# A decoder layer on one core: the feed-forward's products in plain fp32 in place of sums of fp32r parts, last normalisation shared by ACT and DVE

## The reference, cut to what matters

```python
logits = jnp.clip(xt @ gate_w.T, -50.0, 50.0)
top_w, top_idx = jax.lax.top_k(logits, 2)
rw = jax.nn.softmax(top_w, axis=-1)
deltas = jax.nn.softmax(expert_atom_weights, axis=-1) @ atoms
weighted = deltas * jax.nn.sigmoid(importance)          # 8 experts x 2048
rows, cols = mask_idx // H, mask_idx % H                # 2048 indices
vals = jnp.einsum('tk,tks->ts', rw, weighted[top_idx])
contrib = jax.ops.segment_sum((xt[:, cols] * vals).T, rows, num_segments=H)
out = xt @ W.T + contrib.T
x = _layernorm(x + out)
```

## Time and profile before

| | us |
|---|---|
| median of 3 runs | 961.38 (958.9 to 964.02) |
| the profiled execution's own time | 964.11 |
| its span in the profile | 962.3 |
| cross attention, last batch | about 850 to 884 |
| feed-forward phase | 886.3 to 962.3 |
| mean granted clock, share of 2.4 GHz | 0.959 |

### The profile page before, as it was taken

One profiled execution on the slowest core, in us unless ns is written; L12 is line 12 of the kernel. 1 busy time (PEld: TensorE's weight loads), 2 busy tenths in 40 slices (PEclk: granted clock), 3 DMA queues, 4 the chain that ended last, 5 costly groups with the idle time before them and its releaser, 6 DMA issues. The chain is left out here.

```text
span 962.3 us, 19095 instructions
## 1 busy us (share of the span) xinstructions
PE 876.3 (91%) x7675; PEld 760.0 (79%) x7675; DVE 564.5 (59%) x1073; ACT 551.5 (57%) x948; POOL 85.7 (9%) x96
## 2 busy tenths in 40 slices
PE   5944689999999999999999999999999999997875
PEld 3533479898889888988898889898989898976654
DVE  2796455656565656565656565656565656565764
ACT  2512166757576657665666566656665667565322
POOL 1021000000000000000000000000000000016577
PEclk8966799999999999999999999999999999999997
DMA  6009566675757575757575757575757575454042
GB/s 177 12 30 265 148 136 161 133 176 128 177 117 181 126 181 119 177 127 179 118 178 127 179 118 178 128 178 118 179 125 181 117 178 107 97 145 127 20 118 75
DMA packets 70262, 133.32 MB, mean 139 GB/s; under 512 B 24096, under 2 KB 53448, under 8 KB 70088
## 3 DMA queue, kind: packets, MB, share of 16 engines
q1 hardware_dynamic: 66240, 123.61, 54.1%
q0 software_dynamic: 2048, 7.34, 2.8%
q10 hardware_dynamic: 1888, 1.15, 0.4%
HBM read 52.59 MB, written 5.57 MB: 60 GB/s over the span
## 5 line engine op out<-in xcount | busy, mean ns | idle before, releaser
L1267 ACT ACTIVATE probsT<-ps_T 125x448 f32<-125x448 f32 x384 | 195.1, 544 | 176.4 <-PE ps_T L1141 176.3
L1370 DVE CUSTOM_DVE_ANT_0 scores<-ps_scores,mask_sb 112x1500 f32<-112x1500 f32 x128 | 219.7, 1716 | 79.0 <-PE ps_scores L1130 71.1
L1141 PEld LDWEIGHTS ps_T<-ident,scores 112*125 112x125 f32 x1536 | 199.9, 188 | 18.9 <-ACT probsT L1267 4.7
L1141 PE MATMUL ps_T<-ident,scores 112*125 112x112 f32 x1536 | 207.5, 271 | 2.9 <-ACT probsT L1267 2.7
L1257 ACT ACTIVATE scores<-scores,shift 112x1500 f32<-112x1500 f32 x128 | 197.1, 1540 | 1.5 <-DVE shift L1370 1.5
L1118 PE MATMUL ps_proj<-wkvT,room 128*125 128x256 f32 x1152 | 159.7, 289 | 5.9 <-DVE v_sb L1348 5.9
L1110 PE MATMUL ps_proj<-room,wkvT 128*128 128x500 f32 x576 | 157.2, 409 | 5.5 <-DVE room L1353 3.8
L1155 PE MATMUL ps_out<-probsT,v_sb 125*32 125x112 f32 x3072 | 159.6, 260 | 0.0
L1118 PEld LDWEIGHTS ps_proj<-wkvT,room 128*125 128x125 f32 x1152 | 146.8, 189 | 14.7 <-DVE v_sb L1348 6.1
L1155 PEld LDWEIGHTS ps_out<-probsT,v_sb 125*32 125x32 f32 x3072 | 144.2, 110 | 15.5 <-issue 10.7
L1357 DVE SCALAR_TENSOR_TENSOR room<-ps_proj,xbk,room 128x500 fp32r<-128x500 f32 x96 | 70.8, 738 | 125.6 <-ACT room L1252 125.6
(11 more groups left out here) (254 smaller groups left out, 561.7 us busy)
## 6 DMA issues: line engine op xcount, KB each, us to landing
k_stack<-room SPq DMA_DIRECT2D x384, 187.5 KB, 4.0
ctx_rows<-in_ctx SPq DMA_DIRECT2D x48, 500.0 KB
mask_sb<-in_mask_BxSxS_ff SPq DMA_DIRECT2D x32, 328.1 KB
q_stack<-q_hi SPq DMA_DIRECT2D x32, 112.0 KB, 5.4
q_hi<-k_stack SPq DMA_DIRECT2D x4, 448.0 KB, 3.8
q_lo<-k_stack SPq DMA_DIRECT2D x4, 448.0 KB, 4.0
q_stack<-q_lo SPq DMA_DIRECT2D x16, 112.0 KB, 5.4
x_sb<-in_x SPq DMA_DIRECT2D x1, 896.0 KB, 6.9
```

Source lines behind the costliest of these rows:

```text
L1141: last = nc.tensor.transpose(ps_T[0:LT, (TB * t + k) % 2, j * PN:(j + 1) * PN], scores[:, t % 2, (k * TC + j) * LT:(k * TC + j + 1) * LT], ...
L1267: nc.scalar.activation(probsT[:, t % 2, k * TC:(k + 1) * TC], ps_T[0:LT, (TB * t + k) % 2, 0:TC * PN].rearrange("p (j n) -> p j n", j=TC), ...
L1370: nc.vector.tensor_tensor_reduce(out=split(scores[:, t % 2], NC), in0=ps_scores[0:PN, :, 0:LC], in1=split(mask_sb[:, a], NC), scale=-1.0, ...
```

## The change

- The high and low parts of `W`, of the gate weights, of the transposed tokens and of `prod` are gone. `wT`, `gateT`, the tokens `x2T` and `prod` are plain fp32, and `pick_r` is read as fp32. `scatter` has two products in place of four, `dense` four in place of twelve, the logits two in place of six.
- ACT's rounding copies, POOL's and DVE's low parts, and the two low parts of weights at the start of the cross attention (DVE) are gone. T is one DVE copy; ACT stores the tokens once it is done. In the last batch of the cross attention that store stands behind the next probability copies.
- POOL's gathers of the second half stand directly behind the power of the last tile.
- `centre` is a `scalar_tensor_tensor` with `rstd` broadcast as second operand.
- The last normalisation: DVE computes `shift = -mean * rstd` (`shifted`), ACT centres the four tiles of the first half and two of the second with it, DVE the other two. The output goes in three stores: the first half and two tiles from SP's queue, two tiles from ACT's.

The core of the diff:

```diff
     elif u == ("L", 0, 0):
-        (hi, lo), g_hi, g_lo = x2T_parts(keep, h), keep["gateT_hi"], keep["gateT_lo"]
-        mm = [t for m in range(KT) for t in ((g_hi[:, m], hi[:, m]), (g_hi[:, m], lo[:, m]), (g_lo[:, m], hi[:, m]))]
-        for n, (g, x) in enumerate(mm):
-            last = nc.tensor.matmul(bank[0:E, 0:HALF], g, x, start=n == 0, stop=n == len(mm) - 1)
+        for m in range(KT):
+            last = nc.tensor.matmul(bank[0:E, 0:HALF], keep["gateT"][:, m], x2T_of(keep, h)[:, m], start=m == 0, stop=m == KT - 1)
...
     elif kind == "T":
-        dve.wait_ge(k["x2T_hi_ready"], KT * h + p + 1)
-        hi, lo = x2T_parts(keep, h)
-        nc.vector.tensor_tensor(lo[:, p], bank[:, 0:HALF], hi[:, p].bitcast(F32), ALU.subtract).then_inc(out, 1)
+        nc.vector.tensor_copy(x2T_of(keep, h)[:, p], bank[:, 0:HALF]).then_inc(out, 1)
...
-    nc.vector.tensor_scalar(keep["x1"][:, tile], keep["resid"][:], keep["mv"][:, 0:1], keep["rstd"][:, bass.ds(tile, 1)],
-                            ALU.subtract, ALU.mult).then_inc(keep["r_steps"], 2)
+    nc.vector.scalar_tensor_tensor(out=keep["x1"][:, tile], in0=keep["resid"][:], scalar=keep["mv"][:, 0:1],
+                                   in1=keep["rstd"][:, tile:tile + 1].broadcast_to([TT, D]),
+                                   op0=ALU.subtract, op1=ALU.mult).then_inc(keep["r_steps"], 2)
...
             def _(pool):
                 nc.gpsimd.memset(keep["c_stack1"][:].bitcast(F32), 0.0).then_inc(keep["stack_cleared"], 1)
-                for n in range(NST):
-                    low(n)
-                    if n == POW_AT:
-                        result_on_gpsimd(nc, pool, keep, NT - 1)
+                result_on_gpsimd(nc, pool, keep, NT - 1)
                 pool.wait_ge(keep["x2T_stored"][1], 16)
                 for j in range(NST):
                     pool.wait_ge(prod_ready, j + 1)
                     gather_on_gpsimd(nc, pool, io, keep, 1, j)
-                for n in range(NST, len(UNIT)):
-                    low(n)
...
-                        mm = [t for k in range(KT) for t in ((wT_hi[:, k, e], x2T_hi[:, k]), (wT_hi[:, k, e], x2T_lo[:, k]),
-                                                             (wT_lo[:, k, e], x2T_hi[:, k]))]
-                        for n, (w, x) in enumerate(mm):
-                            nc.tensor.matmul(ps[:, 4 + 2 * h + m, 0:HALF], w, x, start=n == 0, stop=False)
+                        for k in range(KT):
+                            nc.tensor.matmul(ps[:, 4 + 2 * h + m, 0:HALF], wT[:, k, e], x2T_of(keep, h)[:, k], start=k == 0, stop=False)
...
                 def scatter(n):
                     h, j = UNIT[n]
-                    wait_lo(pe, n)
+                    pe.wait_ge(prod_ready, n + 1)
                     for m in range(KT):
-                        for part in (prod_hi, prod_lo):
-                            last = nc.tensor.matmul(ps[:, 4 + 2 * h + m, 0:HALF], pick_r[:, j, m * P:(m + 1) * P], part[:, n % BUFS],
-                                                    start=False, stop=j == NST - 1 and part is prod_lo)
+                        last = nc.tensor.matmul(ps[:, 4 + 2 * h + m, 0:HALF], pick[:, j, m * P:(m + 1) * P], prod[:, n % BUFS],
+                                                start=False, stop=j == NST - 1)
                     last.then_inc(contributed, 1)
...
+                def centred(h, which):
+                    act.wait_ge(shift_ready, h + 1)
+                    for i in which:
+                        nc.scalar.activation(y_sb[:, i], resid3[:, i], ACT.Identity, scale=rstd[:, i:i + 1], bias=shift3[:, i:i + 1]).then_inc(y_ready[2 * h], 1)
+                copied(0)
+                centred(0, tiles(0))
                 copied(1)
+                centred(1, tiles(1)[HT // 2:])
+                act.wait_ge(y_ready[2], HT // 2)
+                store(act, tiles(1)[HT // 2:])
...
                         if n >= BUFS:
-                            wait_lo(dve, n - BUFS)
+                            dve.wait_ge(contributed, n - BUFS + 1)
                         nc.vector.tensor_tensor(prod[:, n % BUFS], ps[:, 2 + n % 2, 0:HALF], xg[j], ALU.mult).then_inc(prod_ready, 1)
-                        if n > 0:
-                            low(n - 1)
```

More of the change, by code:

```diff
@@ L649, in load_indices, with store_transposed @@
                  allow_slow_non_contiguous=True).then_inc(keep["idx_col_in"], 16)
-def store_transposed(act, io, keep, h):
-    act.wait_ge(keep["x2T_full"], KT * (h + 1))
-    act.dma_start(io["x2T"][h].rearrange("(m p) t -> p m t", p=P), expert_room(keep)["x2T"][:, KT * h:KT * (h + 1)]).then_inc(keep["x2T_stored"][h], 16)
+def store_transposed(act, io, keep, h, out, out_value):
+    act.wait_ge(out, out_value)
+    act.dma_start(io["x2T"][h].rearrange("(m p) t -> p m t", p=P), x2T_of(keep, h)).then_inc(keep["x2T_stored"][h], 16)
 def gather_on_gpsimd(nc, pool, io, keep, h, j):
@@ L772, in late_unit_on_vector @@
     k = keep
-    if kind in "RL" and read:
+    if kind in "RTL" and read:
         dve.wait_ge(in_psum, in_value)
@@ L1288, in batch @@
                         probs_out(2 * d + 1)
+                        if at is AT_LAST and d == 0:
+                            store_transposed(act, io, keep, 0, unit_out, units_before(half, a) + AT_LAST[("T", KT - 1, 0)] + 1 + 2)
                         next_exponentials(2 * d)
@@ L1594, in feed_forward_phase @@
         sem = lambda n: ctx.enter_context(nc.semaphore(n))
[L1595 to L1596 removed]
         keep["c_stack1"] = sb("c_stack1", [P, HALF], F32R)
         e = expert_room(keep)
[L1599 to L1600 removed]
+        pick, xg = e["pick_r"].bitcast(F32), e["xg"]
+        wT, w_stack, x2 = (keep[n] for n in ("wT", "w_stack", "x1"))
         prod = sb("prod", [P, BUFS, HALF])
[L1602 to L1603 removed]
         ffT = sb("ffT", [P, KT, T])
@@ L1626, in feed_forward_phase @@
         rstd_ready = sem("rstd3_ready")
-        y_ready = [sem(f"y_ready{h}") for h in range(2)]
+        shift_ready = sem("shift3_ready")
+        y_ready = [sem(f"y_ready{n}") for n in range(3)]
         stored = keep["stored"]
@@ L1631, in tiles, with store @@
             return range(h * HT, (h + 1) * HT)
-        def on_pool(n):
-            return n < NST or n >= POOL_FROM
-        def lo_before(n, pool):
-            return sum(on_pool(k) == pool for k in range(n))
-        def wait_lo(engine, n):
-            if on_pool(n):
-                engine.wait_ge(lo_pool, lo_before(n, True) + 1)
-            else:
-                engine.wait_ge(lo_dve, lo_before(n, False) + 1)
+        def store(engine, which):
+            out = io["out"].rearrange("b s d -> (b s) d").rearrange("(i p) d -> p i d", p=TT)
+            engine.dma_start(out[:, which[0]:which[-1] + 1], y_sb[:, which[0]:which[-1] + 1]).then_inc(stored, 16)
         with nc.Block() as block:
@@ L1652, in _ @@
                 stack_shares(sp, keep, 1, late_out, len(HIDDEN))
-                for h in range(2):
-                    sp.wait_ge(y_ready[h], HT)
-                    sp.dma_start(io["out"].rearrange("b s d -> (b s) d").rearrange("(i p) d -> p i d", p=TT)[:, h * HT:(h + 1) * HT],
-                                 y_sb[:, h * HT:(h + 1) * HT]).then_inc(stored, 16)
-                sp.wait_ge(stored, 32)
+                sp.wait_ge(y_ready[0], HT)
+                store(sp, tiles(0))
+                sp.wait_ge(y_ready[1], HT // 2)
+                store(sp, tiles(1)[:HT // 2])
+                sp.wait_ge(stored, 48)
             @block.gpsimd
@@ L1691, in dense @@
                 def dense(h):
-                    x2T_hi, x2T_lo = x2T_parts(keep, h)
                     if h == 1:
@@ L1818, in normalise, with shifted @@
                     nc.vector.tensor_scalar(var_eps[:, g], mv[:, g, 1], LN_EPS, None, ALU.add).then_inc(var_ready, 1)
-                def centred(h):
+                def shifted(h):
+                    g = slice(h * HT, (h + 1) * HT)
                     dve.wait_ge(rstd_ready, h + 1)
-                    for i in tiles(h):
-                        nc.vector.tensor_scalar(y_sb[:, i], resid3[:, i], mv[:, i, 0:1], rstd[:, i:i + 1], ALU.subtract, ALU.mult).then_inc(y_ready[h], 1)
+                    nc.vector.scalar_tensor_tensor(out=shift3[:, g], in0=mv[:, g, 0], scalar=-1.0, in1=rstd[:, g], op0=ALU.mult, op1=ALU.mult).then_inc(shift_ready, 1)
                 def late(k):
                     late_unit_on_vector(nc, dve, keep, HIDDEN[k], 1, ps[:, k % 2], NT - 1, late_in_psum, k + 1, late_out, k + 1)
-                def low(n):
-                    if not on_pool(n):
-                        dve.wait_ge(prod_hi_ready, n + 1)
-                        if n >= BUFS:
-                            dve.wait_ge(contributed, n - BUFS + 1)
-                        nc.vector.tensor_tensor(prod_lo[:, n % BUFS], prod[:, n % BUFS], prod_hi[:, n % BUFS].bitcast(F32), ALU.subtract).then_inc(lo_dve, 1)
                 late(0)
@@ L1854, in _ @@
                             normalise(0)
```

(7 more changed lines are left out.)

97 lines of the change are left out of this document (24 added, 73 removed).

## The result

The changed kernel took 970.52 us (median of 4 runs, 968.51 to 972.87), the kernel before beside it 960.73 (4 runs): ratio 1.0087, 95% interval 1.0058 to 1.0117, so 8.4 us slower; the two medians are 9.8 us apart. The forecast was 967.1, 5.7 us more than the profiled execution of before; the time lies in the range given, and the sign is the forecast one. The profiled execution of the changed kernel has a span of 966.7 us, 4.4 more than that of before (own times 968.51 and 964.11; the first is the fastest of its runs, the second stands above its median, so the pair of profiles shows less than the medians do). Executions more than 1.5% above the fastest of their kernel are left out of every ratio and of the medians of the kernel before.

A forecast was written before the change was run, and what follows sets the result against it. No engine filled the feed-forward; its chain of waits did, and PE would fill it after the change. Terms 0.3 + 0.7 + 5.1 - 0.4 = +5.7 us on 961.4 gave 967.1 us, range 962.5 to 972.

The forecast's parts named there:

- The bound: Feed-forward to its last scatter: no engine fills it, waits do; after the change PE should run gapless.
- The price of a product: One plain fp32 128x448 product on PE: 0.753 us, taken from self-attention; each replaced fp32r pair costs 0.343 us more.
- The rival of 0.820: Plain fp32 products on PE take four fp32r passes, 0.820 us each, or loads show: 971.9 us; chance 0.12.
- the fast one of 0.376: Plain fp32 products on PE cost one record, 0.376 us, not two: 944 us; chance 0.05.
- 1, the last batch: Last batch of cross attention: logits go from six fp32r products to two fp32 ones on PE, +0.3 us.
- 2, to the end of `dense(0)`: Start of the feed-forward to the end of `dense(0)`: four fp32 products are 16 passes, +0.7 us.
- about 10 in the 3.7 us until the clock rises: In `dense(0)`: about 10 of 16 passes before the clock rises, 6 more at 0.188, 1.1 us.
- the clock rival: Feed-forward start: clock rise one step earlier costs 2 us less, 965 us; later, 969 us; chance 0.16.
- 3, to the last scatter: From the end of `dense(0)` to the last scatter: PE work 61.3 plus waits 1.0, 62.3 against 57.2, +5.1 us.
- The three checks of "gapless": PE up to the last scatter: gathers early, DVE's 3.14 us block covered by 3.4, no wait for PSUM or `prod` buffers.
- 4, the tail: After the last scatter: centrings split over DVE and ACT gain 0.4 us, stores still 3.2 us; -0.4 us.
- The hand-over of `shift`: After the last scatter: `shift` adds a small DVE operation and a hand-over, 0.2 us.

The follow-up runs named there:

- the second experiment: Changed kernel with scatter back to hi/lo fp32r products, high parts by ACT, all low parts by DVE, POOL only gathers and powers: 980.6 us, ratio 0.9951.

## Why the prediction came out as it did

*The bound.* Right. The kernel was filled by nothing and is now filled by PE (62.37 of 63.00 us). The rule of the sum, added PE work against waits that vanish, is what the runs bear out: with the scatter alone taken back to fp32r parts the loss turned into a gain, 11.0 us between the two in one group, and the intervals of the ratios (0.9933 to 0.9969, 1.0045 to 1.0084) are apart.

*The price of a product.* Right: 1.50 us for the two of a unit, 0.75 each, against 0.753 from the earlier trace rows. The rival of 0.820 is out, and so is the fast one of 0.376. The Trainium skill (FP8 and Floating Point Precision, TensorE Precision Notes) says four passes; the trace shows two records of 0.376 each for a product, against 0.205 for an fp32r product. So four passes at the fp32r pace don't give the time here: a quarter of 0.753 is 0.188, shorter than 0.205.

*1, the last batch* (+0.3). Wrong in what it covers. PE's last products there started 0.7 us later, at 881.59 instead of 880.90, but the phase began 0.8 us earlier. The sum took the gathers to be finished before the barrier and PE's end to set it. By the two lines of the last gather and the kernel before's second profile, the phase starts 3.4 to 3.6 us after the last issue each time, while PE waits: 2.93 us before, 1.41 now and 4.22 in the second profile of before. So PE's added 0.3 us could not show, and the term that counted, when POOL issues its last gather, stood in the sum at nothing. It moved by 2.0 us between two profiles of the kernel before, so the -0.8 need not be the change's.

*2, to the end of `dense(0)`* (+0.7). Wrong by 0.9: it took 7.5 us, not 8.4. The sum put the rise of the clock inside 893 to 894; the profile shows 0.69 in 890 to 891 and 1.00 from there. The step that failed is "about 10 in the 3.7 us until the clock rises". This is the clock rival (0.16), in one profile; it gave back less than the 2 us that I gave it. (The sum's own terms, 3.7 and 1.1, make 4.8; the 0.2 up to 5.0 is not worked out.) In the first group the changed kernel ran `dense(0)` at the full clock, 1.00 in each microsecond from 898 on, after a wait of 0.74 us at the barrier:

```profile
903.60 3.17 PE L1642 MATMUL psC<-ctx_rows,wfT 128*128 128x448 f32 x8
```

So the same program met the start of the phase at different clocks, 3.96 and 3.17 us for the same eight records, as the rival said.

*3, to the last scatter* (+5.1). It was +6.0: 63.1 us and not 62.3. The 1.60 us of the logits instead of 1.5, and values that take 0.40 instead of 0.20 behind small pieces (907.91 and 911.84 in the chain of waits), make 0.5 us of the 0.8; the other small pieces took 1.8 us and not 1.6, and `back(0)` 0.87 and not 0.8. The waits were about as allowed: 0.58 in the profile, and the value behind it starts 0.52 us after the one before instead of 0.20. The three checks of "gapless" held: the first gather came at 906.54, 4.5 us before the 911 I gave, DVE's block from 937.09 to 940.24 cost PE nothing, and DVE never waited for a buffer. In the second experiment, where two units in hand are 2.04 us, the same block did cost 2.17. That the gathers could have come later without harm was argued, and the run with late gathers does not settle it.

*4, the tail* (-0.4). It was -0.5. The hand-over of `shift` was sized right (0.2), ACT's two centrings were not: 1.09 us and not 0.75. What made up for it are the stores, 2.4 and 2.8 us to land instead of 3.2.

```profile
out<-y_sb SPq DMA_DIRECT2D x1, 224.0 KB, 2.4
out<-y_sb ACTq DMA_DIRECT2D x1, 224.0 KB, 2.8
```

*The sum.* +5.7 forecast; +4.4 between the two profiles; by the ratio +8.4 in the first comparison and +6.4 in the repetition. Between the profiles the four terms missed by -1.1, -0.9, +0.9 and -0.1: that they partly cancel is luck, and the first two hang on the last gather and on the clock. What was forecast for a reason, and came, is the stretch of the scatters. The time of 970.52 lies 3.4 us above the forecast, more than the terms explain. Executions of one kernel in that comparison differ by 4 to 5 us, and the two profiled ones lie at opposite ends, which may be why the profiles and the runs don't agree better; no run shows it.

## What to carry to other kernels

Price an engine's work from start to start of records of the same form elsewhere in the trace, and then ask whether the engine that gets the work has room; here 22 us of PE work were to buy some 16 us of waiting, and did not pay. Where waits come from one misplaced job (POOL's low parts ahead of its gathers), move the job: the second experiment took the waits without the dearer product and was 0.3 to 0.5% faster than the kernel before in three groups. And at a barrier ask which engine arrives last: a term for another one cannot show.

## What was not expected of the hardware

**One DVE operation stood as long as POOL worked.** DVE's centring of the last tile in the kernel before, all eight of its kind, and the low parts of POOL around the last one:

```profile
L870 DVE TENSOR_SCALAR x<-resid_x,mv_x,rstd_x x8: 403/404/3096, 294.5 to 899.2; 112x256 f32<-112x256 f32 x8
```

```profile
898.76 3.34 POOL L1668 TENSOR_TENSOR k_stack<-prod,k_stack 128x448 fp32r<-128x448 f32 x3
```

```profile
899.15 3.10 DVE L870 TENSOR_SCALAR x<-resid_x,mv_x,rstd_x 112x256 f32<-112x256 f32 x1
```

It takes 0.40 us seven times and 3.10 the eighth, until the third of three low parts is done (902.10). With the operation changed to L857 and POOL's low parts kept, it took 3.24 (first line, low parts on POOL); with DVE's low parts 0.48 (second line):

```profile
L857 DVE SCALAR_TENSOR_TENSOR x<-resid_x,mv_x,rstd_x x8: 474/477/3240, 294.8 to 912.5; 112x256 f32<-112x256 f32 x8
```

```profile
L857 DVE SCALAR_TENSOR_TENSOR x<-resid_x,mv_x,rstd_x x8: 474/476/480, 296.3 to 914.4; 112x256 f32<-112x256 f32 x8
```

So it goes with POOL's work, not with the form of DVE's operation. The Trainium skill (SBUF — State Buffer, "SBUF: two separate sides") says that an operation of POOL and one of DVE that has two inputs in SBUF, or runs in a two-port mode, share a pair of ports, which the first of them holds for its whole instruction while the other stands. L857 has two such inputs; whether L870 runs in that mode no view shows. The trace agrees that DVE stands, except that here DVE stood through three instructions of POOL in a row, 3.1 us, and not through one of 1.1.

**Idle without a wait beside the gathers, on three of the chips.** In the groups where the kernel before takes 978 to 984 us, PE's last batch ran single products with gaps while POOL issued the sixteen gathers; all of these kernels had the changed code of that phase. The changed kernel in the first group:

```profile
867.36 2.49 PE L1142 MATMUL ps_out<-probsT,v_sb 125*32 125x112 f32 x39
870.31 0.26 PE L1142 MATMUL ps_out<-probsT,v_sb 125*32 125x112 f32 x1 [0.46 <-issue]
871.06 0.27 PE L1142 MATMUL ps_out<-probsT,v_sb 125*32 125x112 f32 x1 [0.49 <-issue]
```

Up to 867 us the profiles run alike (the same product starts at 866.53 in the quick one, and has its 48 records without a gap); the feed-forward then starts at 900.95 instead of 885.49. In the second half DVE stood up to 11.78 us (second experiment) until the last gather was out, and with late gathers the stretch came later too. What holds the engines up was not found; with the limit of four gathers the feed-forward started some 5 us earlier, and the stretch did not go away. Since the kernel before also takes some 20 us more in those groups, it probably meets both kernels, but its trace on such a chip was not taken.
